# Delta-rule attention between two feed-forward blocks: the engines' call orders found anew, one sign kept, one product moved to GpSimd

## The reference

```python
w = bg[..., None] * kg                      # beta * k, R = 4 keys a token
M = tril(k_i * exp(G_t - G_s) . w, k=-1)    # decayed products of keys with keys
kexp = kg * exp(Gg)
rhs = vg - kexp @ S
u = solve_triangular(M, rhs, lower=True, unit_diagonal=True)
qhat = qg * exp(Gg)
o = SCALE * (qhat @ S + attn @ u)
kdec = w * exp(glast - Gg)
S = exp(glast) * S + kdec^T @ u
```

## Time and profile before

| | us |
|---|---|
| median of 3 runs | 5047.38 |
| lowest and highest | 5040.43 and 5057.70 |
| the profiled execution's own time | 5033.69 |
| its span, first to last instruction | 5031.9 |

### The profile page before, as it was taken

How to read it: one execution, slowest core, us unless ns; L and a number is a source line. 1 busy time by engine, 2 the same in 40 slices (tenths; PEclk the granted TensorE clock), 3 DMA queues, 4 the chain that set the end, 5 groups by cost and what they waited for, 6 DMA issues and landing times.

```text
span 5031.9 us, 151432 instructions
## 1 busy us (share of the span) xinstructions
PE 4536.7 (90%) x63200; PEld 3150.7 (63%) x63200; DVE 4129.7 (82%) x7262; ACT 3477.7 (69%) x6775; POOL 3212.0 (64%) x5316
## 2 busy tenths in 40 slices
PE   8869999999999999999999999899999999989888
PEld 5436666666666666666666666666666666666655
DVE  3278998889988899988999888888898988888522
ACT  3267777777777777777777777777777777777431
POOL 0047777777777777777777777667777777767500
PEclk9989999999999999999999999999999999999789
DMA  2110000000000000000100000000000000000100
GB/s 90 61 48 24 25 25 25 18 20 25 34 31 29 13 25 25 25 25 14 33 31 29 25 15 24 25 25 24 19 29 25 25 25 15 24 25 9 36 9 21
DMA packets 49724, 135.45 MB, mean 27 GB/s; under 512 B 7056, under 2 KB 28176, under 8 KB 48400
## 3 DMA queue, kind: packets, MB, share of 16 engines
q1 hardware_dynamic: 49040, 125.77, 7.1%
HBM read 111.60 MB, written 14.16 MB: 25 GB/s over the span
## 4 chain that ended last, share of the span: by engine, by line
PE 55%; DVE 25%; ACT 11%; issue 6%; POOL 1%; DMA 1%; DVEq 0%; SPq 0%; ACTq 0%
PE bank L821 47%; DVE acc L1511 8%; PE bank L291 7%; DVE X L1508 6%; DVE sp_t L1508 2%; ACT L1403 2%; ACT o L1152 2%; ACT Us L1151 2%; DVE Pd L1616 1%; DVE o L1511 1%; DVE Zc L1695 1%; ACT L1438 1%; DVE Rs L1511 1%; PE bank L892 1%; ACT Ztf L1151 1%
## 5 line engine op out<-in xcount | busy, mean ns | idle before, releaser
L1511 DVE SCALAR_TENSOR_TENSOR acc<-bank,vc,acc 128x510 f32<-128x510 f32 (+2 forms) x1728 | 1271.2, 739 | 139.1 <-ACT acc L1151 110.9
L1940 POOL TENSOR_TENSOR LZ<-LZ,LT 128x120 f32<-128x120 f32 (+26 forms) x1984 | 946.4, 477 | 155.5
L1937 POOL TENSOR_TENSOR LT<-LA,LZ 128x120 f32<-128x120 f32 (+26 forms) x1984 | 922.1, 465 | 145.9
L1508 DVE TENSOR_TENSOR X<-KQ,Fl 128x640 f32<-128x640 f32 x1024 | 997.5, 990 | 0.9 <-ACT Fl L1152 0.9
L1910 POOL COPY X<-KQ 128x640 f32<-128x640 f32 x256 | 245.1, 957 | 923.5 <-PE bank L821 315.4
L821 PE MATMUL bank<-X 128*32 128x60 f32 (+1 forms) x32768 | 654.9, 206 | 132.8 <-DVE Pd L1616 86.8
L821 PEld LDWEIGHTS bank<-X 128*32 128x32 f32 x32768 | 528.5, 112 | 365.2 <-issue 207.4
L1151 ACT ACTIVATE Us<-bank 128x128 f32<-128x128 f32 x1024 | 280.1, 275 | 638.2 <-PE bank L821 632.5
L821 PE MATMUL bank<-xnTm,WK 128*128 128x512 f32 x1280 | 651.6, 634 | 47.1 <-DVE acc L1511 33.6
L821 PE MATMUL bank<-Rs,Ztf 128*128 128x128 f32 x2048 | 471.3, 316 | 70.2 <-DVE Rs L1511 49.9
L1889 POOL TENSOR_TENSOR kdec<-KQ,Fe 128x512 f32<-128x512 f32 x256 | 339.4, 1326 | 303.3 <-PE bank L892 303.3
(11 more groups left out here) (145 smaller groups left out, 9364.1 us busy)
## 6 DMA issues: line engine op xcount, KB each, us to landing
WK<-in_wkq SPq DMA_DIRECT2D x64, 704.0 KB, 6.1
WV<-in_wv SPq DMA_DIRECT2D x64, 576.0 KB, 3.8
WO<-in_wo SPq DMA_DIRECT2D x64, 128.0 KB, 2.0
wuh<-in_wu SPq DMA_DIRECT2D x2, 1024.0 KB, 7.4
xt<-in_x SPq DMA_DIRECT2D x4, 512.0 KB, 6.2
wuh_d<-wuh SPq DMA_DIRECT2D x1, 2048.0 KB, 6.3
x_d<-x SPq DMA_DIRECT2D x4, 512.0 KB, 2.9
xnT_d<-xT SPq DMA_DIRECT2D x4, 512.0 KB, 2.7
```

The costliest lines, as they stand in the source:

```text
L1508: return e.tensor_tensor(o, a, b, op)
L1511: return e.scalar_tensor_tensor(out=o, in0=a, scalar=sc, in1=b, op0=op0, op1=op1)
L1937: e.tensor_tensor(tmp, LA[:, j + 1:32, 8 * (j % R) + j // R].unsqueeze(2).broadcast_to([P, rr, cc]), LZ[:, j, 0:cc].unsqueeze(1).broadcast ...
L1940: e.tensor_tensor(LZ[:, j + 1:32, 0:cc], LZ[:, j + 1:32, 0:cc], tmp, SUB).then_inc(g_row, 1)
```

## The change

1. All four call lists are new. The loop's start is another point of the same cycle (what stood last in period p now stands first in p + 1), and within the cycle many calls are moved against each other. Below are the stretches that matter, as they stand after the change.
2. `query` moves from DVE to POOL, without its minus sign, behind most of the `spread` calls. The waits on `v_qn` become waits on `g_qn`; on PE the wait stands ahead of the first product that reads qn, no longer ahead of `update(., ., 0)`.
3. The state is held as S: ADD and SUB change places in DVE's `rhs` and `update`, and ACT's `update` loses its scale of -1, with the same instructions otherwise.
4. `above` writes its result back into the PSUM bank of the decay projection, and `softplus` adds from there. The bank is free when `softplus` is done, no longer when `above` is.
5. POOL's `begin` writes the diagonals in one instruction instead of four.
6. The 30 interleaved units are called one at a time (`DRAIN`): 10 in the recurrence of stage 62 from its fourth chunk on, 8 in the inversion of stage 63, 12 in the recurrence of stage 63. Before, 15 stood in each of the two recurrences, in groups of 3 and 2, and none in the inversion. DVE's first part of phase 3 (`begin(0)`, which needs a DMA) is called later. SyncE issues the load of the last tile ahead of the barrier that ends phase 2.

```diff
+DRAIN = ((2, 10), (2, 11), (2, 13), (2, 14), (2, 16), (2, 17), (2, 19), (2, 20), (2, 22), (2, 23),
+         (1, 30), (1, 31), (1, 32), (1, 33), (1, 34), (1, 35), (1, 36), (1, 37), (1, 1), (1, 2),
+         (1, 4), (1, 5), (1, 7), (1, 8), (1, 10), (1, 11), (1, 13), (1, 14), (1, 16), (1, 17))
-        def drained(s, c):
-            if s == NS - 2 and 3 <= c < 8:
-                u = 3 * (c - 3)
-                return range(min(u, NU), min(u + 3, NU))
-            if s == NS - 1 and 1 <= c < 8:
-                u = 14 + 2 * c
-                return range(min(u if c > 1 else 15, NU), min(u + 2, NU))
-            return range(0)
+        def drained(s, j):
+            for u, (back, k) in enumerate(DRAIN[:NU]):
+                if (NS - back, k) == (s, j):
+                    return [u]
+            return []
...
             def above(s):
-                w.wait_ge(v_C, every(s - 1, 1))
-                act(sp_t[:, :], bank[bank_use["decay", 0, s][0]][:, :], ACT.Relu, bias=dtb[:, h:h + 1]).then_inc(a_relu, 1)
+                raw = bank[bank_use["decay", 0, s][0]][:, :]
+                act(raw, raw, ACT.Relu, bias=dtb[:, h:h + 1]).then_inc(a_relu, 1)
...
             def softplus(s):
-                tt(sp_t[:, :], sp_t[:, :], rn[:, 0, :], ADD).then_inc(v_sp, 1)
+                w.wait_ge(a_F, every(s - 1, 12))
+                tt(sp_t[:, :], bank[bank_use["decay", 0, s][0]][:, :], rn[:, 0, :], ADD).then_inc(v_sp, 1)
...
-            def query(s):                       # VectorE
-                stt(qn[:, s % 2, :].rearrange("p (g t) -> p g t", t=8), KQ[:, s % 2, :, 4, :], -1.0,
-                    Fe[:, 0, :].rearrange("p (g t) -> p g t", t=8), MUL, MUL).then_inc(v_qn, 1)
+            def query(s):                       # GpSimd
+                w.wait_ge(v_kq, every(s, 1))
+                w.wait_ge(a_F, nth(s, 12, 0))
+                w.wait_ge(p_o, every(s - 2, 16))
+                e.tensor_tensor(qn[:, s % 2, :].rearrange("p (g t) -> p g t", t=8), KQ[:, s % 2, :, R, :],
+                                Fe[:, 0, :].rearrange("p (g t) -> p g t", t=8), MUL).then_inc(g_qn, 1)
...
-                for k in range(2):
-                    for hf in range(2):
-                        a = 32 * hf + 17 * k
-                        e.tensor_scalar(flat[:, a:a + 463:66], Cn[:, :, 2 * hf + k], half_c[hf], None,
-                                        MUL).then_inc(g_init, 1)
+                e.tensor_tensor(LZd, Cn[:, :, :].rearrange("p t (h k) -> p t h k", h=2),
+                                half_c.unsqueeze(1).unsqueeze(3).broadcast_to([P, 8, 2, 2]), MUL).then_inc(g_init, 1)
```

More of the change, by code:

```diff
@@ L119, in build @@
         one_c = cs[:, C_SMALL + 2:C_SMALL + 3]
-        half_c = [cs[:, C_SEL + 16 + half:C_SEL + 17 + half] for half in range(2)]
+        half_c = cs[:, C_SEL + 16:C_SEL + 18]
         d_cst = sem("d_cst")
@@ L1097, in delta_tensor @@
+                second(p - 2, 0)
+                spare(p - 2, 31)
+                turn_v(p - 2, 0)
+                products(p - 1, 2, 2)
+                turn_v(p - 2, 1)
+                turn(p - 1, 0)
+                third(p - 2, 0)
+                spare(p - 2, 32)
+                turn_v(p - 2, 2)
                 products(p - 1, 2, 3)
-                turn_v(p - 2, 1)
                 products(p - 1, 2, 4)
-                third(p - 2, 0)
-                turn_v(p - 2, 2)
-                turn(p - 1, 0)
+                total(p)
@@ L1112, in delta_tensor @@
-                products(p - 1, 3, 3)
+                spare(p - 2, 35)
                 solve(p - 2, 0, 0)
                 products(p - 1, 3, 4)
-                project_k(p + 1, 0)
+                update(p - 2, 0, 0)
+                turn(p - 1, 2)
                 third(p - 2, 1)
-                update(p - 2, 0, 0)
+                spare(p - 2, 36)
                 project_k(p + 1, 1)
-                fourth(p - 2, 1)
-                rhs(p - 2, 0, 1)
-                solve(p - 2, 1, 0)
-                solve(p - 2, 0, 1)
@@ new lines, in delta_scalar @@
+                length(p - 2, 0)
+                turned(p - 2, 2)
+                tap_k(p, 1)
+                update(p - 3, 0, 0)
+                factors(p - 1, 2)
+                spare(p - 3, 36)
+                fourth(p - 3, 1)
+                spare(p - 3, 37)
+                solve(p - 3, 1, 0)
+                spare(p - 3, 1)
+                update(p - 3, 1, 0)
+                spare(p - 3, 2)
+                solve(p - 3, 0, 1)
+                factors(p - 1, 3)
+                tap_k(p, 2)
@@ L1414, in delta_scalar @@
+                solve(p - 3, 0, 6)
+                decay(p, 1)
+                above(p)
+                solve(p - 3, 1, 6)
+                decay(p, 2)
+                silu_k(p, 2)
+                spare(p - 3, 19)
+                spare(p - 3, 20)
+                solve(p - 3, 0, 7)
+                solve(p - 3, 1, 7)
+                tap_k(p, 3)
+                out_square(p - 3)
+                silu_v(p - 1, 0)
+                keep(p - 1, 0)
                 e.preload_act_table_set("natural_log_exp_and_others")
@@ new lines, in delta_vector @@
+                spare(p - 3, 30)
+                spare(p - 3, 31)
+                spare(p - 3, 32)
+                spare(p - 3, 33)
+                spare(p - 3, 34)
+                spare(p - 3, 35)
+                spare(p - 3, 36)
+                spare(p - 3, 37)
+                spare(p - 3, 1)
+                rhs(p - 3, 0, 1)
+                distance(p - 1, 4)
+                conv_k(p, 1, 1)
+                spare(p - 3, 2)
+                rhs(p - 3, 1, 1)
+                update(p - 3, 0, 1)
@@ new lines, in delta_vector @@
+                conv_k(p, 1, 0)
+                conv_k(p, 2, 2)
+                spare(p - 3, 4)
+                rhs(p - 3, 0, 2)
+                levels(p - 1, 0, 1)
+                update(p - 3, 1, 1)
+                conv_k(p, 2, 1)
+                spare(p - 3, 5)
+                rhs(p - 3, 1, 2)
+                conv_v(p - 1, 0, 2)
+                spare(p - 3, 7)
+                update(p - 3, 0, 2)
+                update(p - 3, 1, 2)
+                spare(p - 3, 8)
+                rhs(p - 3, 0, 3)
@@ L1802, in delta_vector @@
[L1802 to L1803 removed]
+                softplus(p)
+                spare(p - 3, 20)
                 rhs(p - 3, 1, 7)
[L1805 to L1807 removed]
+                add_up(p)
+                diagonal(p - 2)
                 conv_k(p, 3, 2)
                 conv_k(p, 3, 1)
+                conv_k(p, 3, 0)
+                evacuate(p - 1, 0, 0)
+                levels(p - 1, 1, 3)
```

435 lines of the change are left out of this document (208 added, 227 removed).

## The result

The changed kernel is **slower by 0.64%**: 5073.57 us (median of 5 runs, 5070.48 to 5084.51) against 5041.86 us (median of 5 runs of the kernel before, on the same chip); the ratio is 1.0064, with a 95% interval of 1.0047 to 1.0080. The forecast was 4925 us, and 5074 lies outside its range. The profiled execution took 5084.51 us, with a span of 5082.6 us.

The account below looks back on a forecast made before the run. PE, ACT and DVE were taken to hold the chain in turn. -2.6 + 0.75 + 0.6 - 0.45 = -1.7 us a period, -107 over 63, and -16 for the drain gave 4925 us; range 4810 to 5040.

Parts of the forecast that it names:

- What bounds the kernel: A 69.36 us period is a stretch of PE's (44.6 us), one of ACT's (4.0) and one of DVE's (20.9).
- DVE's stretch, -2.6: From `gated` to the end of evacuate(2,3): softplus and levels 3,2 leave, clamp and evacuate(0,3) enter, -2.6 us a period.
- (c): Rival, chance 0.18: slower, 5088 us; evacuate(0,3) behind `gated` 0 makes PE wait 0.5 to 1.2 us at products(1,0), again at products(2,0).
- (d): Rival: more POOL products meet DVE's levels and distance, 1.0 us each; about 5031 us, chance 0.12 shared with the gain-given-back rival.
- ACT's stretch, +0.75: Between out_square and out_root: silu_v, keep's copies and a length's first step enter, decay 2 leaves; +0.75 us a period.
- PE's stretch, +0.6: The fourth `turn_v` enters the part of the period where PE holds the chain: +0.6 us a period.
- POOL, nothing: Diagonals in one instruction (-1.6 us) and the moved product (+1.3) on POOL: nothing on the path, between -1 and +1.
- PE's waits, -0.45, between +1 and -2: In PE's stretch, mostly a projection or product now stands between a solve and its update: -0.45 us a period.
- The clock: PE's granted clock, read as 0.99 in the steady part; no term of the period's sum was given to it.
- The drain, -16: End of the run: interleaved units fill the last inversion (-12), DVE's xt wait (-3) and last tile's load (-1): -16 us.
- The filling, nothing: Start of the run, 208 to 415 us: same dependences from another loop start, nothing, within 5 us.
- (b): Rival: the 2.6 us are given back at the next joint, PE waiting at products(2,0) or (3,0); 5031 us, shared chance 0.12.

Follow-up runs that it names:

- a_evac: The changed kernel with VectorE's evacuate(p-1,0,3) ahead of gated(p-3,0) instead of behind it: 5069 us, ratio 1.0057 to the kernel before.
- b_small: The kernel before, own order and loads, with only the state's sign kept, the query product on GpSimd and the diagonals in one instruction: 5038 us, ratio 0.9986.
- a_copy: The changed kernel without the repeated table load; ACT copies the turned keys (2) out three times instead of once: 5065 us, ratio 1.0046.
- a_turn: The changed kernel with ACT's turned(p-2,2) ahead of the repeated table load and length(p-2,0), load kept: 5220 us, ratio 1.0344.
- a_move: The changed kernel with the repeated table load moved from the head of ACT's period to directly ahead of factors(p-1,3): 5105 us, ratio 1.0111.
- a_noload: The changed kernel with the repeated table load at the head of ACT's period left out in the 62 steady periods: 4944 us, ratio 0.9811.

## Why the prediction was wrong, by its own steps

**What bounds the kernel:** right for the kernel before. The periods without a fall of the clock, cut in three (means in us), show what became of each term:

| kernel | mean square to `gated` | `gated` to the end of evacuate(2,3) | the rest, mostly PE's stretch | sum |
|---|---|---|---|---|
| before | 3.22 | 20.82 | 45.20 | 69.24 |
| changed | 3.86 | 20.54 | 45.29 | 69.69 |
| before, load left out | 3.22 | 20.82 | 44.44 | 68.49 |
| changed, load left out | 3.86 | 20.51 | 43.84 | 68.21 |
| forecast of the change | +0.75 | -2.6 | +0.15 | -1.7 |

**DVE's stretch, -2.6: the step that failed.** It became shorter by 0.28 us, not by 2.6. The pieces did what was said. The addition in `softplus` takes 0.69 instead of 1.75 (tile view of the changed kernel, to be read beside the earlier trace rows):

```profile
L1544 DVE TENSOR_TENSOR sp_t<-bank,rn x64: 683/685/693, 265.4 to 4685.5; 128x512 f32<-128x512 f32 x64
```

What the sum put at nothing is that DVE now waits for PE inside the stretch, for 2.4 us ahead of `evacuate(2, 0)` (mean; 2.17 in the rows above). The prediction had named the limit ("until PE's own stream there is the later one") and not worked it out. Up to the end of `products(2, 4)` PE needs 22.3 us from the mean square on, where it was 18.0. The new list puts a third `turn_v`, a `turn` and `third` ahead of it, 2.3 us of work, and PE's waits up to there are 3.0 us in place of 0.9. End of `products(2, 4)` and start of `products(3, 0)` on PE, before and after:

```profile
2535.39 0.75 PE L821 MATMUL bank<-X 128*32 128x80 f32 x16
```
```profile
2582.55 1.03 PE L825 MATMUL bank<-X 128*32 128x40 f32 x32
```
```profile
2585.63 0.91 PE L825 MATMUL bank<-X 128*32 128x60 f32 x64
```

So `products(3, 0)` start 24.3 us behind the mean square, with no wait ahead of them, and before they started 24.1 us behind it, with a wait of 1.42. The waits of 1.26 and 0.65, which the prediction had priced in its rival (c) and left out of its own sum, are part of PE's 3.0; moving `evacuate(0, 3)` alone did not bring `evacuate(2, 0)` forward (`a_evac`), and which call would have to move was not tried. By the table this term is 2.3 us a period short, 146 us over 63 periods, the most of what was missed. The sum also left out `lengths`, which now stands ahead of evacuate(2,3) as well (0.2 us); that is small beside the rest.

**By the Trainium skill** ("GPSIMD Engine Reference", section 8, "Key points") DVE instructions with two SBUF inputs contend with GpSimd. The trace of after agrees, with the operand in PSUM as the way out: 0.69 at most in all 64, whatever POOL does. Case (d), more such meetings, did not come: the mean of X fell from 0.99 to 0.91 us.

**ACT's stretch, +0.75:** from out_square's start (2560.55) to `gated` (2565.16) 4.61 us, against 3.96; +0.65. **PE's stretch, +0.6:** PE's busy time in periods without a fall went from 63.26 to 63.72, +0.46. **POOL, nothing:** right in the old order (`b_small`); the diagonals take 0.70 in one, the product 1.31.

**PE's waits, -0.45, between +1 and -2:** the second step that failed, though the table hides it: the rest of a period is +0.09 where the sum had +0.15. Without the load in either kernel it is -0.60; the load costs 45.29 - 43.84 = 1.45 us there in the new order and 0.76 in the old one, and this took the gain away. The place was looked at from PE's list alone ("mostly a projection or a product stands between"). Such a projection helps only if its bank is free, and the bank of `project_k(p, 2)` hangs on ACT, behind a load that the new list has at its head. ACT's list was read behind `out_square` and nowhere else. The new wait is 1.73 us each period.

**The clock:** no term at all. The granted clock of 0.99 in the steady part was taken for a constant. It costs 0.5 us a period before and 1.2 after.

Together, by the medians: a change of -122 us was forecast and +32 was measured, 154 apart. The load accounts for 61 of them, since it costs 130 us in the new order and 69 in the old one, and the forecast had no price for either. Without the load in either kernel the change gives 28 us, 94 too few. That is the 146 of the DVE term, less some 47 by which the rest of the period without the load (-0.60) was better than its term. That the kernel without the load stands at 4944 us, near the forecast of 4925, is luck: it has lost 69 us that the load cost in the old order too, which no step of the prediction counts on.

**The drain, -16:** from the 62nd mean square to the end 333.7 us before and 321.3 after, -12.4; right. The other profiled kernels of the old order have 339.2 and 339.7 there, those of the new order 320.2 to 322.9. PE is busy over 90% in the last inversion, as forecast (94%, at a clock of 0.91; before, 64% at 0.68):

```profile
4886.70:4927.80 41.10, 38.69 (x327) 26.51 (x327) 3.92 (x7) 16.32 (x27) 0.00 (x0) 0.91 0.08 27
```

**The filling, nothing:** the first mean square is at 435.0 in both.

**The rivals.** (c) had the waits of 1.26 and 0.65 right in place and about in size, and the sign of the result, but not its cause: `a_evac` gave back 4 us. Its 5088 is the nearest number, and the prediction gave it a chance of 0.18 and left it out of its range. (b) had it right that the 2.6 us are given back; they are given back one joint earlier than it said, with DVE waiting for PE ahead of `evacuate(2, 0)`. Neither had the load or the clock.

The Trainium skill's "ScalarE: Activation LUTs" says, in "Table sets: the hidden batching unit", that a pass of the compiler's back end puts a load ahead of every activation that needs one. The runs agree: with the explicit load left out, its 68 loads become 6, those that the compiler adds stay at 196, and the kernel takes 4944 us. The same page of the Trainium skill, in "What ACT_TABLE_LOAD costs", gives 1283 ns for the load, which is the trace's mean of all of them. It adds about 1380 ns of drain at a switch to another set; the trace of the changed kernel shows none around the load that stands behind `silu_v` 0 and ahead of `length` 1 (from 2562.21 to 2563.49, with the next activation at 2563.50).

## What to carry to other kernels

When work is taken out of one engine's stretch, look up for each wait inside the stretch when the other engine lets it go in the new order: here DVE gave up 2.6 us of calls and got back 2.4 of waiting.

In a hand-ordered pipeline read, for each engine, what stands ahead of the call that frees the next operand or bank of the bounding engine: an instruction without an output (a table load) is in no data dependence and yet holds up all behind it, and leaving it out may be worth more than its time. Where the bounding engine is PE, count the waits of over a microsecond by their place; each may be followed by a stretch at the lower clock, on top of its length. Before an order is judged, take out what is superfluous in both versions, or the order's own effect (here -28 us) drowns in what the surplus costs in each (69 and 130 us).

## What the hardware showed that was not expected

- A load of a table set that is already in is executed, 1.28 us each time. Two directly in a row were one in the trace.
- The granted clock fell to half 0.7 to 1.5 us behind waits of PE of 1.5 to 1.7 us in the periods read: 25 to 46 falls at that place in 60 periods (the changed kernel, `a_evac`, `a_copy`, `a_turn`, `a_move`), although PE is busy 92% of the time. It did not fall once within 4 us behind the wait of 1.26 us ahead of products(1,0). In the kernel before, 7 of the 18 falls begin 24 to 31 us behind the mean square, from the wait of 1.42 us on, and 10 right behind the mean square, at its waits of 0.78 and 0.44. So the length of a wait alone doesn't tell; what else does was not tried.
- Two to eight falls are left in each kernel of the new order 18 to 23 us behind the mean square, `a_noload` too. They were not looked into.
- 1.8 us of useless PE work a period, put where PE would wait, made a kernel 42 us faster.
- In the changed kernel a period with 3.4 us at the lower level took 71.02 us (mean of 34), against 69.69 without (20): 0.39 us lost for each us at the lower level. If PE's work alone set the time it would be 0.5, by the two levels (an estimate).
